# Eight small expert gates become one; copies, casts, x and the first y of a chunk at other tiles

## What is computed

```python
xp = xn @ in_proj_w.T + in_proj_b;  u, v = split(xp, 2)
delta = softplus(u @ delta_proj_w.T)
B = (u @ b_proj_w.T + b_proj_b)                 # 8 groups x 16 states
u_conv = silu(causal_conv(u, conv_w, conv_b))   # 4 taps
h = exp(delta * A) * h + (delta * u_conv) * B   # a scan over 2048 steps, 1024 x 16 states
y = sum_n(h * c_param) * silu(v)

shared = swiglu(xn @ w_shared_in) @ w_shared_out
probs = softmax(xn @ w_gate + gate_bias);  top_val, top_idx = top_k(probs, 2)
routed = sum_e wdense[:, e] * (swiglu(xn @ w1_shared) @ w2[e])
out = x + y + shared + routed
```

## Time and profile before

| | |
|---|---|
| median of 3 runs | 2282.99 us (2276.42 to 2293.36) |
| the profiled execution | 2270.09 us; spans of the cores 2238.6 to 2268.5 us |
| busy in the span of 2268.5 us | PE 77%, DVE 78%, ACT 58%, POOL 65% |
| granted PE clock, by core | 0.865 to 0.889 of full speed |
| DMA | 559.8 MB, mean 247 GB/s |
| start of tile 0, 128, 256, 384 | 100.9, 432.6, 719.5, 1031.1 us |
| start of tile 512, 640, 768, 896 | 1275.4, 1513.3, 1756.3, 2003.8 us |
| end of the last scan | 2257.6 us |

### The profile page before, as it was taken

One profiled execution on the slowest core, in us unless ns is written; L12 is line 12 of the kernel. 1 busy time (PEld: TensorE's weight loads), 2 busy tenths in 40 slices (PEclk: granted clock), 3 DMA queues, 4 the chain that ended last, 5 costly groups with the idle time before them and its releaser, 6 DMA issues.

```text
span 2268.5 us, 34928 instructions; the slowest of 8 cores (2238.6 to 2268.5 us)
## 1 busy us (share of the span) xinstructions
PE 1752.5 (77%) x8659; PEld 738.3 (33%) x8659; DVE 1769.2 (78%) x2114; ACT 1315.5 (58%) x2077; POOL 1480.8 (65%) x1347
## 2 busy tenths in 40 slices
PE   6637888598878877777799779987998789754664
PEld 2213333233333333233344334433443334311221
DVE  5239767689888898979878668866986888676997
ACT  3325346554677565364567656764676656564774
POOL 0326455456556545456889768886888778695995
PEclk9757787779989989888899989988999999976777
DMA  8799997788778888555899899989998999788986
GB/s 195 183 234 245 226 244 201 205 241 235 217 231 264 233 251 212 139 157 180 272 299 284 266 303 303 307 263 281 294 309 268 313 276 249 240 268 272 269 239 203
DMA packets 131226, 559.80 MB, mean 247 GB/s; under 512 B 24018, under 2 KB 33618, under 8 KB 88658
## 3 DMA queue, kind: packets, MB, share of 16 engines
q1 hardware_dynamic: 91396, 373.77, 54.5%
q0 software_dynamic: 26096, 153.91, 28.0%
q10 hardware_dynamic: 13536, 29.89, 3.8%
HBM read 486.98 MB, written 122.16 MB: 269 GB/s over the span
## 4 chain that ended last, share of the span: by engine, by line
PE 29%; DMA 26%; DVE 15%; issue 14%; SPq 5%; ACT 5%; POOL 4%; DVEq 1%; ACTq 0%; POOLq 0%
DVE hsc L1224 7%; DMA acc<-x 7%; PE pw L695 6%; PE pw L721 5%; PE pw L682 4%; PE pw L627 3%; DMA part<-acc 3%; DMA ddscr<-dd 3%; PE pw L727 3%; POOL dBu L1294 3%; DMA xt<-x 3%; DMA bb<-bscr 2%; PE pw L643 2%; DMA ring<-wsb 2%; SPq L1361 2%
## 5 line engine op out<-in xcount | busy, mean ns | idle before, releaser
L1294 POOL TENSOR_TENSOR dBu<-rep,bb 128x512 bf16<-128x512 bf16 x1024 | 1176.2, 1163 | 586.4 <-DVE hsc L1224 538.2
L1224 DVE TENSOR_TENSOR_SCAN hsc<-pdA,st,dBu 128x512 bf16<-128x512 f32 x768 | 958.6, 1275 | 143.8 <-ACT pdA L889 83.3
L889 ACT ACTIVATE pdA<-rep,A_sb 128x512 f32<-128x512 bf16 x1024 | 695.5, 687 | 582.1 <-DVE hsc L1224 555.0
L1224 DVE TENSOR_TENSOR_SCAN hsc<-pdA,dBu 128x512 bf16<-128x512 f32 x256 | 304.0, 1214 | 112.5 <-POOL dBu L1294 66.3
L721 PE MATMUL pw<-xn_r,ring 128*128 128x512 bf16 x928 | 259.5, 432 | 95.7 <-DVE acc L1016 47.8
L682 PE MATMUL pw<-ring,area 128*128 128x512 bf16 x1024 | 274.8, 417 | 50.0 <-DMA ring<-wsb 17.6
L695 PE MATMUL pw<-ring,area 128*128 128x512 bf16 x1024 | 247.3, 385 | 32.9 <-ACT area L791 11.2
L804 ACT ACTIVATE th<-pw 128x512 f32<-128x512 f32 x256 | 150.1, 589 | 108.7 <-PE pw L645 34.7
L707 PE MATMUL pw<-xn_r,ring 128*128 128x512 bf16 x512 | 145.5, 436 | 34.5 <-DVE sv L978 15.8
L721 PEld LDWEIGHTS pw<-xn_r,ring 128*128 128x128 bf16 x928 | 95.6, 107 | 231.8 <-issue 168.6
L682 PEld LDWEIGHTS pw<-ring,area 128*128 128x128 bf16 x1024 | 101.9, 104 | 193.4 <-issue 127.3
(11 more groups left out here) (160 smaller groups left out, 1934.1 us busy)
## 6 DMA issues: line engine op xcount, KB each, us to landing
ring<-wsb SPq DMA_DIRECT2D x126, 1024.0 KB
rep<-ddscr SPq DMA_DIRECT2D x256, 256.0 KB
bb<-bscr SPq DMA_DIRECT2D x256, 128.0 KB
orow<-area ACTq DMA_DIRECT2D x78, 256.0 KB
wsb<-ring SPq DMA_DIRECT2D x17, 1024.0 KB, 26.0
ddscr<-dd SPq DMA_DIRECT2D x256, 64.0 KB
acc<-x SPq DMA_DIRECT2D x8, 2048.0 KB, 21.6
wexb<-wex POOLq DMA_DIRECT2D x16, 1024.0 KB, 13.3
```

Source lines behind the costliest of these rows:

```text
L889: sc.activation(pdA[:, j % 2, :], rep[:, G % 2, n % 4, 0, :], AF.Exp, scale=A_sb[:, G % 8, n:n + 1]).then_inc(s_da, 1)
L1224: v.tensor_tensor_scan(hsc[:, n, :], pdA[:, j % 2, :], dBu[:, j % NDB, :], init, ALU.mult, ALU.add).then_inc(s_scan, 1)
L1294: gp_.tensor_tensor(dBu[:, j % NDB, :], rep[:, G % 2, n % 4, 1, :], bb[:, G % 2, n // 4, :], ALU.mult).then_inc(s_dbu, 1)
```

## The change

Five things change.

- **Gate.** GT only adds the bias and puts the logits of its chunk into `lg`, now 128 x 256 for all chunks. Behind the last GT (slot 333), `largest` (slot 336), one `gexp` (337) and one `gate` (338) do the chain once for everything. `eq`, `gp2` and `ohs` lie in `xt`, whose first half is free then.
- **Expert copies** (`wex`) at tiles 140, 156, ..., 380.
- **First-use casts** two tiles later, as far as they don't stand at the floor of -4 or before: 13, 22, 31, 40, 57, 74, 77, and one in the prologue, from -29 to -27.
- **`xacc`** at slot 128 c + 23 of SP instead of 25.
- **YT** of each chunk's first group four slots later: PE 16 G + 32, DVE 16 G + 34.

```diff
@@ build_plan
-        put(16 * G + 15 + LAGY + (3.9 if G == 8 * NCH - 1 else 9.9), ("YT", G // 8, G % 8, 0, None, 0))
+        put(16 * G + 15 + LAGY + (3.9 if G == 8 * NCH - 1 else 13.9 if G % 8 == 0 else 9.9), ("YT", G // 8, G % 8, 0, None, 0))
@@ event tables
-    + [(gslot(("GT", c, 0, 0)) + 3, ("gexp", c)) for c in range(NCH)]
+    + [(gslot(("GT", NCH - 1, 0, 0)) + 4, ("gexp",))]
...
-    + [(gslot(("GT", c, 0, 0)) + 4, ("gate", c)) for c in range(NCH)]
+    + [(gslot(("GT", NCH - 1, 0, 0)) + 3, ("gmax",)), (gslot(("GT", NCH - 1, 0, 0)) + 5, ("gate",))]
...
-POOL_EV += [(60 + 21 * p, ("wex", p)) for p in range(2 * E)]
+POOL_EV += [(140 + 16 * p, ("wex", p)) for p in range(2 * E)]
...
-            POOL_EV.append((max(_t + 3, -4 if _use > 5 else -60) if _t > -40 else -58 if _id in (P_DL, P_DL + 1) else _t,
+            POOL_EV.append((max(_t + 5, -4 if _use > 5 else -60) if _t > -40 else -58 if _id in (P_DL, P_DL + 1) else _t,
                             ("cast", _p)))
...
-    _SP.append((128 * _c + 25 if _c else 4, ("xacc", _c)))
+    _SP.append((128 * _c + 23 if _c else 4, ("xacc", _c)))
@@ tiles
-        lg = T("lg", [128, 4, 8], F32)
-        gp = T("gp", [128, 4, 8], F32)
-        eq = T("eq", [128, 4, 8], F32)
-        gp2 = T("gp2", [128, 4, 8], F32)
+        lg = T("lg", [128, NT, 8], F32)
...
-        ohs = T("ohs", [128, NT + 1, 8], BF16)
...
+        eq = xt[:, 0, 0:8 * NT].rearrange("p (i e) -> p i e", e=8)
+        gp2 = xt[:, 0, 256:256 + 8 * NT].rearrange("p (i e) -> p i e", e=8)
+        ohs = xt[:, 0, 768:768 + 4 * NT + 4].bitcast(BF16).rearrange("p (i e) -> p i e", e=8)
@@ ScalarE, event gexp
-                        c = ev[1]
-                        sc.wait_ge(s_gt, c + 1)
-                        sc.activation(gp[:], lg[:], AF.Exp).then_inc(s_ga, 1)
+                        sc.wait_ge(s_gt, 1)
+                        sc.activation(lg[:], lg[:], AF.Exp).then_inc(s_ga, 1)
@@ VectorE, group GT
-                        lgf = lg[:]
-                        ins = v.tensor_tensor(
-                            lgf, ps[:, 0:32].rearrange("p (i e) -> p i e", i=4),
-                            bgt_sb[:].unsqueeze(1).broadcast_to([128, 4, 8]), ALU.add)
-                        ins.then_inc(s_vev, 1)
-                        v.wait_ge(s_vev, V_IDX[g] + 1)
-                        link(v.tensor_reduce(gc1[:], lgf, AX.X, ALU.max))
-                        v.tensor_tensor(lgf, lgf, gc1[:].unsqueeze(2).broadcast_to([128, 4, 8]),
-                                        ALU.subtract).then_inc(s_gt, 1)
+                        v.tensor_tensor(
+                            lg[:, 4 * c:4 * c + 4, :],
+                            ps[:, 0:32].rearrange("p (i e) -> p i e", i=4),
+                            bgt_sb[:].unsqueeze(1).broadcast_to([128, 4, 8]), ALU.add
+                            ).then_inc(s_vev, 1)
@@ VectorE, the new functions (the chain of gate() goes on as before, each operation on all of lg, oh1, oh2)
+                def largest():
+                    v.wait_ge(s_vev, V_IDX[GI[("GT", NCH - 1, 0, 0)]] + 1)
+                    link(v.tensor_reduce(gc1[:], lg[:], AX.X, ALU.max))
+                    v.tensor_tensor(lg[:], lg[:], col(gc1[:]), ALU.subtract).then_inc(s_gt, 1)
+
+                def gate():
+                    rk = rank8[:].unsqueeze(1).broadcast_to([128, NT, 8])
+                    v.wait_ge(s_ga, 1)
+                    need(v, "DVE", s_xn, 4 * NCH)
+                    link(v.tensor_reduce(gc1[:], lg[:], AX.X, ALU.add))
+                    link(v.reciprocal(gc2[:], gc1[:]))
+                    link(v.tensor_tensor(lg[:], lg[:], col(gc2[:]), ALU.mult))
...
```

More of the change, by code:

```diff
@@ L488, in build @@
         ej = xt[:, 1, D - NBK:D]
-        gc1 = T("gc1", [128, 4], F32)
-        gc2 = T("gc2", [128, 4], F32)
+        gc1 = T("gc1", [128, NT], F32)
+        gc2 = T("gc2", [128, NT], F32)
         hid = area[:, 0:D].rearrange("p (i d) -> p i d", i=2)
@@ L663, in group @@
                         oh = ohb[:].rearrange("p i e -> p (i e)")
-                        sm = ohs[:].rearrange("p i e -> p (i e)")
+                        sm = ohs.rearrange("p i e -> p (i e)")
                         t.matmul(ps[:, 0:8 * NT], ltri[:], oh, start=True, stop=False)
@@ L1035, in group @@
                     ins.then_inc(s_vev, 1)
[L1037 to L1044, removed]
-                    link(v.reciprocal(gc2[:], gc1[:]))
[L1046 to L1051, removed]
-                    o1, o2 = oh1[:, 4 * c:4 * c + 4, :], oh2[:, 4 * c:4 * c + 4, :]
-                    link(v.tensor_tensor(o1, eq[:], col(gc2[:]), ALU.is_ge))
-                    link(v.scalar_tensor_tensor(
-                        gp2[:].rearrange("p i e -> p (i e)"), o1.rearrange("p i e -> p (i e)"),
-                        -4.0, gp[:].rearrange("p i e -> p (i e)"), ALU.mult, ALU.add))
-                    link(v.tensor_reduce(g2, gp2[:], AX.X, ALU.max))
-                    link(v.tensor_tensor(eq[:], gp2[:], col(g2), ALU.is_ge))
-                    link(v.tensor_tensor(eq[:], eq[:], rk, ALU.mult))
-                    link(v.tensor_reduce(gc2[:], eq[:], AX.X, ALU.max))
-                    link(v.tensor_tensor(o2, eq[:], col(gc2[:]), ALU.is_ge))
-                    link(v.tensor_tensor(ohb[:, 4 * c:4 * c + 4, :], o1, o2, ALU.add))
@@ new lines, in col @@
+                def col(x):
+                    return x.unsqueeze(2).broadcast_to([128, NT, 8])
+                def largest():
[7 more added lines that the diff above has]
+                    link(v.tensor_reduce(gc1[:], lg[:], AX.X, ALU.add))
+                    link(v.reciprocal(gc2[:], gc1[:]))
+                    link(v.tensor_tensor(lg[:], lg[:], col(gc2[:]), ALU.mult))
+                    g1, g2 = gw[:, 0, :], gw[:, 1, :]
+                    link(v.tensor_reduce(g1, lg[:], AX.X, ALU.max))
+                    link(v.tensor_tensor(eq, lg[:], col(g1), ALU.is_ge))
+                    link(v.tensor_tensor(eq, eq, rk, ALU.mult))
+                    link(v.tensor_reduce(gc2[:], eq, AX.X, ALU.max))
+                    link(v.tensor_tensor(oh1[:], eq, col(gc2[:]), ALU.is_ge))
+                    link(v.scalar_tensor_tensor(
+                        gp2.rearrange("p i e -> p (i e)"), oh1[:].rearrange("p i e -> p (i e)"),
+                        -4.0, lg[:].rearrange("p i e -> p (i e)"), ALU.mult, ALU.add))
+                    link(v.tensor_reduce(g2, gp2, AX.X, ALU.max))
+                    link(v.tensor_tensor(eq, gp2, col(g2), ALU.is_ge))
+                    link(v.tensor_tensor(eq, eq, rk, ALU.mult))
+                    link(v.tensor_reduce(gc2[:], eq, AX.X, ALU.max))
+                    link(v.tensor_tensor(oh2[:], eq, col(gc2[:]), ALU.is_ge))
+                    link(v.tensor_tensor(ohb[:], oh1[:], oh2[:], ALU.add))
@@ L1201, in event @@
                         token_table()
+                    elif ev[0] == "gmax":
+                        largest()
                     elif ev[0] == "gate":
-                        gate(ev[1])
+                        gate()
                     else:
```

## The result

| | before | after |
|---|---|---|
| median of the runs beside each other | 2279.70 us (2262.89 to 2293.36, 4 runs) | 2244.36 us (2234.35 to 2264.65, 4 runs) |
| ratio | | 0.9877, 95% interval 0.9828 to 0.9926 |
| the same kernel measured again, later | 2283.01 us (17 runs) | 2254.69 us (6 runs), ratio 0.9869 (0.9828 to 0.9910) |

So the change is worth 1.2 to 1.3%, some 30 us (17 to 39 by the first interval), where 56 were forecast. The time lies in the range, but just above the forecast's own band (2195 to 2243), in that of rivals (a) and (d).

The account below looks back on a forecast made before the run. DMA was taken to set the pace in tiles 55 to 128, DVE in 128 to 416 with PE close behind; -27 (y), -18 (gate), -18 +4 (copies), +3 (casts) made -56, from 2283.0 to 2227 us, range 2195 to 2262.

Parts of the forecast that it names:

- (a): Whole kernel: parts hide one another, saved DVE time only uncovers PE (gate 0 to 6); 2251 us; chance 0.22 with (d).
- (d): Chunk starts: edits of x do nothing, YT's wait only moves four tiles on; 2254 us; chance 0.22 with (a).
- y: 27 us forecast: Chunk starts, YT four tiles later: 6 us from chunks 1 to 3, 15 from 4 to 6, 6 from 7.
- What is done in that time is gained: DVE's wait for x at chunk starts: four more tiles done before it, 7.2 us, count as gain.
- (b): Whole kernel: DMA is the bound, x lands later, waits keep their end; 9 us gained, 2274 us; chance 0.13.
- Gate: 18 forecast: One gate instead of eight: 18 us gained, bounds -3 and 29, mostly DVE time of chunks 2 to 6.
- two thirds: Gate: share taken of the 29 us upper bound, as DVE and PE take turns in the chain.
- Copies: 18 less 4 forecast: Expert copies from tile 140: 18 us gained where they leave the crowded stretch, 4 lost in tiles 140 to 380.
- little of it can show: Tiles 140 to 380: 37 us more DMA time with 23% free in 665 us costs only 4 us.
- (c): Tiles 140 to 380: copies collide with `rep` and `bb` loads, POOL waits; 34 us slower, 2317 us; chance 0.05.
- Casts: 3 us lost forecast: First-use casts two tiles later: pieces at tiles 72 and 75 land later for PE; bounds 6 gained, 10 lost.
- x: 0 forecast: Load of x at slot 23: no gain, since it waits for the landing of the old sums' store anyway.

Follow-up runs that it names:

- the variant without chunk 7: Kernel before with only the first y of each chunk four tiles later in chunks 0 to 6, chunk 7 as before: 2278.14 us, ratio 0.9951.

## Why the prediction was right in part

**Direction, range and the sum of parts: right, the last in part by luck.** The parts alone make -0.54 (gate), -0.55 (copies), -0.48 (y), +0.38 (casts) and +0.13% (x), -1.06% in all, and the full change is -1.23 and -1.31%. Each part is uncertain by some 0.3%, so the sum by about 0.7%: the missing half of the gain is already missing in the parts, but a small mutual effect can't be told.

Stage by stage there is one. From tile 144 to 288 the copies alone lost 16.7 us and the gate alone won 7.4, yet the full change won 5.5 (4.1 in its second profile). The wait for x of 21.1 us that the copies alone had there (mean of the cores) is 2.5 us in the full change, whose y comes four tiles later; by tile 384 some of that is lost again. So the edits of y and of the copies belong together, and that the parts add up is in part luck. Rival (a) came nearest in time (2251 us), but not by its mechanism: the gate alone gave 12 us, not 0 to 6, and PE is busy for 75% of tiles 128 to 416, no more than before. Of the single terms only that of y is outside what its run allows (3 to 19 us); gate and copies are judged by their waits.

**y: 27 us forecast, 11 measured.** The waits at L1011 in chunks 4 to 7 are 10.1, 6.7, 9.5 and 6.1 us on the mean of the cores, as the forecast's 5 to 11 had it (core 7 alone has one of 2.3), and x lands 1.2 to 2.9 us later, as forecast.

The step that failed is "What is done in that time is gained". In chunk 7 6 us were counted, and 0 came: the next in line, the addition of partial sums (RG) at tile 941, stands 101.9 us behind the chunk's start (core 7), where it stood at 103.5 before without a wait. In the earlier trace rows that wait was invisible behind the wait for x. In chunks 4 to 6 5 each were counted; in the full change it was 3, 5 and 4 (dBu's wait for `bb` and the x that lands later, as in rival (b) in small). The 6 us of chunks 1 to 3 came and went: in the variant without chunk 7 5.1 us are won from tile 144 to 160 and lost by 192, where DVE waits for ACT and PE, and 3.9 won by tile 416 are lost by 512; the 4.3 of chunk 2 are those that the edit of x gives as well, and half of them are gone by tile 336. Rival (d) was too dark, (b) described the mechanism.

**Gate: 18 forecast, 12 measured.** Right was the price of a gate: 18.8 us of busy time and the gaps between went with four gates, tiles 144 to 336. The lump was 9.5 us; the rows after, DVE's lines L1039 and L1047 (lengthened) and L1059 and L1049 (not; the last has one input only):

```profile
L1039 DVE TENSOR_TENSOR lg<-lg,gc 128x256 f32<-128x256 f32 x1 | 1.2, 1161 | 0.1
L1047 DVE TENSOR_TENSOR lg<-lg,gc 128x256 f32<-128x256 f32 x1 | 0.7, 708 | 0.1
...
L1059 DVE TENSOR_TENSOR xt<-xt,rank_sb 128x256 f32<-128x256 f32 x1 | 0.4, 424 | 0.1
...
L1049 DVE TENSOR_REDUCE gw<-lg 128x32 f32<-128x256 f32 x1 | 0.4, 420 | 0.1
```

L1039 takes 1.16 and L1047 0.71 us, the others of this size 0.42: the first two-input operations are lengthened, the later ones are not, as the rows before had it. Each of the two ends 0.28 us after a dBu of POOL does (POOL is busy with dBu from 865.76 to 866.91 and from 868.53 to 870.86 us, then idle to 879.66). By the rule of the Trainium skill (SBUF — State Buffer, SBUF: two separate sides) a DVE operation with two SBUF inputs and a GpSimd operation that reads SBUF exclude each other for a whole instruction. The trace agrees, but as POOL soon has no dBu left to compute, the rule touches two of the ten such operations. Mis-sized was "two thirds": of the 25.6 us of four gates a third came. And from tile 336 to 384 6.3 us were lost where 3.2 were counted. DVE at 88% busy was read as the bound, but waits for x and for `pdA` end at a transfer's time, and DVE only comes to them earlier.

**Copies: 18 less 4 forecast, 13 measured; the first term right, the second not.** That the sum of 14 agrees is luck of the measurement's width (5 to 20). In the profile 20.5 us were won by tile 144 (18 forecast), but 16 lost up to tile 288 instead of 4. (The forecast's 9.2 us of DMA time for a copy should be 7.4: the 5.24 MB of the earlier trace rows are five pieces, as a cast issued at 242.71 us falls into the window.) The bounds said 0 to 37; the choice "little of it can show" for a stretch with 23% of DMA free was the error. Up to tile 384 it is 16.4 us for four copies more, about 4 each, nearly the 5 us that each gave where it was taken away. Rival (c) named the right place, tiles 140 to 380, but the wrong victim: not `rep` and `bb` but the loads of x and HB's matmuls.

**Casts: 3 us lost forecast, 9 measured alone** (interval 1 to 17). But 3 lies in the interval too. PE's waits for cast pieces grew by 13.7 us on core 7 and by 8.7 on the mean, not by 5: beside those cast at tiles 74 and 77 the piece cast at 57 is waited for longer (6.5 us for 1.5), which the forecast had left out. The gain at tile 11's cast was swallowed, as said: tile 16 starts 0.7 us earlier with it alone, tile 48 2.3 us later.

**x: 0 forecast, 0 measured in all, 4 us at one place.** The issue time was the wrong thing to look at; the place in the queue counted.

## What to carry to other kernels

Before a stall is priced, look for the next thing that a transfer ends behind it (here the partial sums eleven tiles on, and `bb` at the next group of 16): a wait whose end is set by a transfer swallows what any engine gained before it, so count the gain only up to the next such wait. Moving a transfer from a crowded stretch to one with a lower mean share is no gain by itself, as the burst here delayed what was in flight at its place, whichever load that was; price it in both places (here 5 us for each one taken away, 4 for each one added; 1.5 to 2.7 where they were moved about within the full change). Late data may be cured by what is queued ahead of it rather than by when it is issued; here that was seen in one place, worth 4 us.

## What the runs showed of the hardware that was not expected

- A mean DMA share of 0.62 to 0.77 hid little room. Four more copies of 1 MB (bf16, from 2 MB of f32) between tiles 144 and 384 went with 16.4 us lost, evenly spaced, and 22.2 us with the copies kept away from x; the loss stood at different instructions (x for the sums; HB's matmuls and x for the layer norm). Single profiles, good to some 5 us.
- One transfer of 1 MB issued ahead of x or behind it went with a load shorter by 4 us (at most 16.3 for 20.3 us for 2 MB, core 7), though both kinds of transfer were issued within 1.5 us.
- With the DMA engines full at a chunk's start, four more tiles done by DVE before its wait went with a longer load of x in chunk 4: 29.5 us in the full change and 29.0 with y alone, for 26.5 before (mean of the eight cores).
